# Writing the product of gate and up into up's PSUM bank, and rounding both of its halves from there

## What is computed

```python
x = x + attn(layernorm(x), Wq, Wk, Wv)
z = layernorm(x)
shared = (silu(z @ sg.T) * (z @ su.T)) @ sd.T
probs = sigmoid(z @ router_w.T + routing_bias)         # top 2 of 8, scores normalised
g, u = silu(z @ gate_w[e]), z @ up_w[e]                # for each expert e
out = x + shared + sum_e w[:, e] * ((g * u) @ down_w[e])
```

## Time and profile before

| | us |
|---|---|
| median of 3 runs | 566.49 |
| lowest, highest | 561.99, 566.75 |
| span of the profiled execution | 555.3 |
| what lies around the span (median minus span) | 11.2 |
| TensorE matmuls busy | 518.0 (93%) |
| VectorE busy | 369.8 (67%) |
| ScalarE busy | 301.0 (54%) |
| GpSimd busy | 288.9 (52%) |

### The profile page before, as it was taken

The page is one execution under the profiler, slowest core; times in us unless marked ns, Lnnn a source line. Parts: engine busy times, 40 slices in busy tenths (PEclk is TensorE's granted clock), DMA queues, the critical chain, the costliest instruction groups (busy, mean ns, idle before and its releaser), DMA issues.

```text
span 555.3 us, 14903 instructions
## 1 busy us (share of the span) xinstructions
PE 518.0 (93%) x4757; PEld 425.5 (77%) x4757; DVE 369.8 (67%) x980; ACT 301.0 (54%) x580; POOL 288.9 (52%) x242
## 2 busy tenths in 40 slices
PE   4889988999999999997999999999999999999992
PEld 3557766788878888886767788888787888888881
DVE  5788998689887878899747555445454454454551
ACT  3989877678777676744233443433343433434341
POOL 4466677668676765857022344452444434434443
PEclk9999999899999999998899999999999999999998
DMA  8799848949694947414465965764846536345443
GB/s 271 201 181 208 178 127 158 217 133 209 161 208 141 194 127 170 155 70 136 131 115 85 98 107 69 103 83 60 108 59 89 73 60 97 55 65 78 62 58 38
DMA packets 139351, 68.55 MB, mean 123 GB/s; under 512 B 114608, under 2 KB 132336, under 8 KB 139280
## 3 DMA queue, kind: packets, MB, share of 16 engines
q1 hardware_dynamic: 126128, 48.84, 43.5%
q0 software_dynamic: 13152, 18.76, 19.4%
HBM read 19.46 MB, written 23.08 MB: 77 GB/s over the span
## 4 chain that ended last, share of the span: by engine, by line
PE 65%; DVE 12%; DMA 8%; SPq 5%; ACT 5%; issue 3%; POOL 1%; POOLq 0%; ACTq 0%; DVEq 0%
PE bank L2216 29%; PE bank L2240 15%; PE bank L2547 4%; PE bank L2322 3%; PE bank L2564 3%; DMA v<-xnrow 2%; PE bank L2625 2%; PE bank L2347 2%; PE bank L2392 2%; DMA xn2t<-xrow 2%; PE bank L2369 2%; PE bank L2640 2%; SPq L405 2%; DMA x<-x 1%; DVE h L1470 1%
## 5 line engine op out<-in xcount | busy, mean ns | idle before, releaser
L2216 PE MATMUL bank<-xn2t,w 128*128 128x256 f16 x1608 | 184.9, 273 | 1.3 <-DVE th L1653 1.1
L2216 PEld LDWEIGHTS bank<-xn2t,w 128*128 (+1 forms) x1608 | 155.2, 98 | 24.3 <-DVE th L1653 2.2
L1644 DVE SCALAR_TENSOR_TENSOR th<-th,bank 128x512 f32<-128x512 f32 x83 | 56.6, 682 | 55.2 <-ACT th L989 54.1
L2240 PE MATMUL bank<-w,h 128*128 (+1 forms) x768 | 91.5, 273 | 0.0
L943 ACT ACTIVATE h<-th 128x512 f16<-128x512 f32 (+1 forms) x69 | 42.9, 622 | 84.6 <-DVE th L1653 78.3
L989 ACT ACTIVATE th<-bank 128x512 f32<-128x512 f32 x83 | 49.2, 593 | 62.1 <-PE bank L2216 47.6
L2240 PEld LDWEIGHTS bank<-w,h 128*128 128x128 f16 x768 | 74.0, 98 | 10.4 <-DVE x L1676 0.3
L866 POOL DMA_INDIRECT out<-p,wm x28 | 43.9, 1569 | 67.2 <-ACT p L1323 27.3
L1470 DVE TENSOR_TENSOR h<-th,h 128x512 f16<-128x512 f32 (+1 forms) x69 | 50.6, 733 | 38.3 <-ACT h L943 38.1
L734 POOL TENSOR_TENSOR w<-wst,w 128x768 f16<-128x768 f32 x36 | 59.1, 1645 | 18.9 <-ACT w L943 18.7
L758 POOL DMA_INDIRECT rows<-xrow,sidx x56 | 56.5, 1009 | 17.0 <-issue 13.3
(11 more groups left out here) (188 smaller groups left out, 808.4 us busy)
## 6 DMA issues: line engine op xcount, KB each, us to landing
wst<-w_all SPq DMA_DIRECT2D x36, 384.0 KB
x<-x SPq DMA_DIRECT2D x8, 512.0 KB, 5.6
out<-x SPq DMA_DIRECT2D x8, 512.0 KB, 4.0
rows<-xrow POOLq DMA_DIRECT2D x1, 1192.5 KB, 6.6
rows<-xrow,sidx POOLq DMA_INDIRECT x56
out<-p,wm POOLq DMA_INDIRECT x28
xn2t<-rows SPq DMA_TRANSPOSE x26
wm<-rows SPq DMA_DIRECT2D x26, 9.0 KB, 2.4
```

The source lines that it names most:

```text
L1644: d.scalar_tensor_tensor(out=tb, in0=tb, scalar=1.0, in1=G[half][:, :], op0=ALU.add, op1=ALU.mult).then_inc(f_sg, 1)
L2216: ins = mm(dst, w_ap(j, ws, m * MAT + k * I + (2 * half + i) * P, P), moving(ms * KD + k), start=(cnt == 0), stop=(cnt == 3 * KD - 1))
L2240: ins = mm(o[:, a * D:(a + 1) * D], hb[:, (hs * KI + i) * TT + a * P:(hs * KI + i) * TT + (a + 1) * P], w_ap(j, ws, 2 * MAT + i * D, D), s ...
```

## The change

`ffn_up` writes the product to `U[half]`, in place, and `split_h` and `ffn_low` read it there. So `th[half]` is free after `f_h`, and `tanh` waits for `f_h` of half n - 2. `U[half]` is free only after `f_lo`: TensorE waits for it before the first matmul into `U` (the wait for `f_h` before `G` stays where it was), and before the value projection. The second half of the last pair waits for `f_lo` too, and keeps its product in `th`; singles and halves are as before.

```diff
@@ -985,7 +985,7 @@
                 if isinstance(t, int) and t < 0:
                     return
                 act.wait_ge(gu_mm, t * 2 + half + 1)
-                wait(act, f_lo, t * 2 - 2 + half + 1)
+                wait(act, f_h, t * 2 - 2 + half + 1)
                 a.activation(th[:, half * 512:(half + 1) * 512], G[half][:, :], ACT.Tanh,
                              scale=0.5 / WS).then_inc(f_tanh, 1)
 
@@ -999,7 +999,7 @@
                     act.wait_ge(dump_in, 16)
                 wait(act, dn_mm, t * 2 - (4 if shared else 2) + half + 1)
                 copy((h_of_tile(t) if shared else h)[:, half * 512:(half + 1) * 512],
-                     th[:, half * 512:(half + 1) * 512]).then_inc(f_hi, 1)
+                     U[half][:, :]).then_inc(f_hi, 1)
 
             def ffn_half(t, half):
 
@@ -1650,8 +1650,8 @@
                     return
                 tb = th[:, half * 512:(half + 1) * 512]
                 dve.wait_ge(f_sg, t * 2 + half + 1)
-                d.scalar_tensor_tensor(out=tb, in0=tb, scalar=0.5 / (WS * WS), in1=U[half][:, :], op0=ALU.mult,
-                                       op1=ALU.mult).then_inc(f_h, 1)
+                d.scalar_tensor_tensor(out=U[half][:, :], in0=tb, scalar=0.5 / (WS * WS), in1=U[half][:, :],
+                                       op0=ALU.mult, op1=ALU.mult).then_inc(f_h, 1)
 
             def ffn_half(t, half):
 
@@ -1664,7 +1664,7 @@
                     return
                 ht_ = h_of_tile(t) if isinstance(t, int) else h
                 dve.wait_ge(f_hi, t * 2 + half + 1)
-                low(ht_[:, (2 + half) * 512:(3 + half) * 512], th[:, half * 512:(half + 1) * 512],
+                low(ht_[:, (2 + half) * 512:(3 + half) * 512], U[half][:, :],
                     ht_[:, half * 512:(half + 1) * 512]).then_inc(f_lo, 1)
 
             def add_shared(t):
@@ -2206,6 +2206,8 @@
                     pe.wait_ge(f_h, t * 2 - 2 + half + 1)
                 for m in mats:
                     o = (G[half], U[half])[m]
+                    if m == 1:
+                        wait(pe, f_lo, t * 2 - 2 + half + 1)
                     for i in range(2):
                         dst = o[:, i * TT:(i + 1) * TT]
                         if shape3:
@@ -2359,7 +2361,7 @@
                     pe.wait_ge(xn0_lo, KD)
                     pe.wait_ge(wv_lo, 1)
                 for m in range(first, last):
-                    wait(pe, f_h, 4 * (b - 3) + 3 + m)
+                    wait(pe, f_lo, 4 * (b - 3) + 3 + m)
                     if b:
                         pe.wait_ge(v_lo, 2 * b - 1 + m)
                     for i in range(2):
@@ -2695,7 +2697,7 @@
 
             def last_gate_up(t, j, moving):
 
-                pe.wait_ge(f_h, t * 2)
+                pe.wait_ge(f_lo, t * 2)
                 pe.wait_ge(ys_read, SINGLES)
                 pe.wait_ge(yh_read, HALVES)
                 for i, banks in enumerate(LAST_CHUNKS):
```

## The result

The changed kernel takes 579.33 us (median of 4 runs, 577.61 to 583.10), the kernel before 564.24 us beside it (4 runs, 560.76 to 566.75): ratio **1.0297, interval 1.0242 to 1.0351**. The forecast was 578.0 us, slower.

The account below looks back on a forecast made before the run. TensorE was taken to bound the routed stage, VectorE the end of the shared stage. Opening 0 + middle 1.0 + end 8.8 + clock 1.7 = 11.5 us, on a 555.3 span with 11.2 around it: 578.0 us, range 569.5 to 584.

Parts of the forecast that it names:

- absorbed: Rival: at the end of the shared stage VectorE hides most of TensorE's lateness; +4.1 us, 570.6 us, chance 0.16.
- faster: Rival: low parts no longer collide with GpSimd operations, giving back 5.5 us; 561.0 us, chance 0.06.
- the clock falls at each new wait: Rival: three drops of TensorE's clock at 2.5 us each on the chain; 583.8 us, chance 0.08.
- The end of the shared stage, step by step: Six steps following how U's waits for low parts delay TensorE and VectorE from half 22 on; +8.8 us.
- step 5: Low part of half 28 takes 0.69 us, ending +4.3; VectorE's addition after tile 13's down product starts +8.6.
- Steps 1 to 4: End of shared stage: U of halves 22, 24, 26, 29 late by 0.86, 3.8, 6.1, 8.65 us; table of quads +7.7.
- the sum's +1.7: TensorE's clock: +1.7 us taken between one drop less (-2.5) and three more (+7.5).
- The opening: U of half 2 comes 3.2 us later, half 3's low part gives back 2.06; 0 taken, bounds -0.7 to +1.6.
- The middle of the stage: Middle of the shared stage: U waits in three batches, losing 0.31, 0.37 and 0.32 us; together +1.0 us.
- The routed stage: TensorE bounds it; at least 2.81 us of room per half hides the price; over 1 us longer would be wrong.
- The median of the runs leaves 11.2 us around it, which stay: Base of the forecast: profiled span 555.3 us, median 566.49; the 11.2 us outside the span remain unchanged.
- The signs it named: New profile: U of half 24 4.8 us later, TensorE idle some 10 us, singles table near 270, low parts under 0.8 us.

Follow-up runs that it names:

- e2: Kernel before with the product kept in SBUF, but TensorE waiting for the low part before U and the value projection: 582.70 us, ratio 1.0419.
- e6: The change for halves 20 to 31 alone, the other halves as in the kernel before: ratio 1.0340.
- e7: Changed kernel with five low parts earlier in VectorE's list and one high part earlier in ScalarE's: ratio 1.0037 to the kernel before.
- e9: Changed kernel with TensorE repeating G's matmuls ahead of the waits at halves 24, 26, 29 and 30: 575.57 us, ratio 1.0205 to before.
- e4: The change for the shared expert's 32 halves alone, routed ones as in the kernel before: 580.25 us, ratio 1.0381.
- e11: Changed kernel with low parts of halves 22, 23 and 24 earlier on VectorE and one high part earlier on ScalarE: ratio 1.0181 to before.
- e10: Changed kernel with GpSimd making the low parts of weight chunks 32 and 33 after batch 7's last four scatters: ratio 1.0220 to before.
- e12: Changed kernel with only the low parts of halves 27 and 28 earlier in VectorE's list: ratio 1.0181 to the kernel before.
- e1: The kernel before, unchanged, run for a second profile: 563.5 us, ratio 0.9961.
- e3: The change for the routed experts' 51 halves alone, shared ones as in the kernel before: ratio 0.9964.
- e8: Kernel before, product in SBUF, with five low parts earlier in VectorE's list and one high part earlier in ScalarE's: ratio 1.0000.

## Why the prediction was right

It forecast a loss by the later release of U, at the end of the shared stage, and the runs show that: e2 has the cost with the waits alone, e6 has it with the last twelve halves alone, and e7 loses it again by moving low parts. The rivals "absorbed" (570.6) and "faster", where low parts no longer collide (561.0), are out. Of the rival "the clock falls at each new wait" (583.8) half is true: three drops came in this stage, but they cost 4.8 us and not 7.5. The time came within 1.3 us, but that close by luck, as the paragraph "Around the span" shows.

**The end of the shared stage, step by step.** e9 is the changed kernel without clock drops there, so it shows the steps by themselves. Shifts are against the kernel before, less the shift of U(20) (5.4 us after, 4.4 in e9):

| point | predicted | e9 | after |
|---|---|---|---|
| U(22) | 0.9 | 0.9 | 1.3 |
| U(24) | 3.8 | 3.8 | 4.3 |
| U(26) | 6.1 | 6.0 | 6.5 |
| U(29) | 8.65 | 8.6 | 10.6 |
| table of quads starts | 7.7 | 8.1 | 11.0 |
| U(30) | 10.5 | 14.4 | 17.3 |
| add_shared(14) | 8.8 | 12.8 | 18.0 |
| U(32) | 10.5 | 12.0 | 17.2 |

(U(30) by step 5: 258.8 + 0.06 - 248.38 = 10.5. U(32) is 8.8 + 1.7 for the clock.) Steps 1 to 4 hold within 0.4 us. **Step 5 failed**: "at 0.69 it ends at 250.37 + 7.7 + 0.69 = 258.8" took the collision for a property of the low part. It belongs to GpSimd's two operations, whose place comes from GpSimd's own list. In all six kernels that are late there (after, e2, e4, e6, e9, e11) they met an operation of the table; in e7, e10 and e12, where the table was done before they began, no operation of VectorE was held up. In e9 it was:

```profile
260.63 3.86 DVE L1773 SCALAR_TENSOR_TENSOR phl<-phl,tneg 1x18 f32<-1x18 f32 x1
```

3.86 - 0.23, its time without a collision (e10), is 3.6 of the 3.9 us by which U(30) is later than forecast. This is a sum; the experiment on it, e10, was spoilt.

**The clock.** The drops behind the new waits came, and cost more than forecast. No run shows the sum's +1.7: it was the author's estimate, between no other figures than multiples of 2.5 us, by which 24 matmuls at a granted clock of 0.50 (5.30 us) last longer than 24 at 1.00 (2.79 us at 284.54 after). Between e9 and after lie 5.2 us (18.0 - 12.8 at add_shared(14)). Of these, 0.5 stand at U(22) already, before the first drop; the other 4.8 are what the drops cost. The prediction also counted on 2.5 us for a drop of the kernel before that would go. It went (granted clock 1.00 from 284.54 to 287.33), but gave back only 0.8, from 18.0 to 17.2 in after and from 12.8 to 12.0 in e9. The first routed gate-up tells why. Before:

```profile
266.20 5.70 PE L2216 MATMUL bank<-xn2t,w 128*128 128x256 f16 x48
```

and after:

```profile
289.17 5.41 PE L2218 MATMUL bank<-xn2t,w 128*128 128x256 f16 x48 [1.84 <-issue]
```

At a granted clock of 1.00 the down product is over sooner (2.79 us against 5.30), but TensorE then waits 1.84 us: the gate-up starts 4.69 us after VectorE's addition ends, against 5.16 with the product at 0.50, and is itself 0.3 us shorter. So the clock's net term is 4.8 - 0.8 = 4.0 us where the sum had 1.7. The step that failed is "nearer to where the new idle times fall short of the 3.14 that the row shows": idle times of 2.25 and 2.29 us were followed by a drop here.

**The opening** was put at 0; it costs 2.7 us (35.5 or 35.6 in the eight profiles with the whole change there, 32.7 to 33.1 in the five without), over its bound of 1.6. U(2) is 3.2 us late as forecast, after an idle time of 3.01 us, and then runs at a granted clock of 0.50 (67.80 to 71.10):

```profile
67.80 5.74 PE L2218 MATMUL bank<-xn2t,w 128*128 128x256 f16 x36 [3.01 <-DVE h L1470]
```

36 matmuls in 5.74 us instead of the 4.10 that such a row takes at 1.00 (233.01 to 237.11): 1.6 us. "Some 1.6 us for what follows it" had no clock in it. 3.2 + 1.6 - 2.05 for the collision is the 2.7 us. "With its full operand in PSUM it should not" is what the traces show: in the kernel before, two low parts whose full operand is a bank took 0.69 us each within a GpSimd operation (the one at 20.55 in 20.25 to 21.90, that at 28.19 in 27.75 to 29.88). Of the two collisions there, that of the low part is won (2.05 us by e2), and the one of `one_hot` stays (2.42 us in both kernels).

**The middle of the stage**: 1.0 forecast. U(4) to U(20) averages 115.3 in the five profiles without the change there (before, e1, e3, e6, e8) and 116.7 in the nine with the new waits, +1.3 (+0.9 without e1), with single ones from 113.8 to 118.0: in agreement, but no closer than that.

**The routed stage** took nothing, as forecast: 0.8 us more from U(32) to the end than in the kernel before, e3 level with e1, 693 ns for the up product.

**Around the span.** "The median of the runs leaves 11.2 us around it, which stay": only 1.8 us lie around it. On the profiled execution as its base the sum would have been 555.3 + 1.8 + 11.5 = 568.6, on a typical one of before (564.24) 575.7. The measured loss is 15.1 us where the steps gave 11.5; of the 3.6 us too few, 2.2 were made up by a first median (566.49) that lay above the later one. That is why the time came out so close. And 15.1 is itself on the small side, for the kernel before was slower beside the changed one (564.24 us) than in the later sets (559.93 to 563.43). e4, whose profile is that of the changed kernel, lost 580.25 - 561.21 = 19.0 us, and from U(0) to U(32) the profiles of after and e4 take 233.0 and 234.2 us against 211.1 to 213.0 in before, e1, e3 and e8, some 21 us. The steps gave little more than half of that: step 5, the clock and the opening are what they lack.

**The signs it named.** No low part takes over 0.8 us (the longest 0.69), the routed stage and the up product stay within their limits. TensorE's idle time ended by low parts came to more than the "some 10 us", 13.8 on the matmul queue alone, and 17.5 with the two called "issue" ahead of halves 22 and 24; the table of singles starts at 284.4 and not near 270.

## What to carry to other kernels

Freeing one buffer early by holding another longer is a trade in release times: compare, for both buffers, when the next user arrives and when the last reader is done. Where a wait is added, first look at the list of the engine that ends it: here the same change cost 3.0% with the low parts where they were and 0.4% with five of them (and one high part) moved ahead of work that could wait, as the kernel before with the same order shows (1.0000). Price a collision by the engine that causes it, not by the operation on which it shows: GpSimd's two operations here last 3.24 us, and held up the low part in the kernel before (4.12 us) and a table operation after (3.62 us). And price a loss of clock by what waits behind it: 2.5 us lost in a product were worth 0.8 where another wait stood next.

## What the runs showed of the hardware

- TensorE's granted clock fell to 0.50 after idle times of 2.25 to 3.01 us and not only after 3.14; also after 2.11 (e12, before 263.10), 2.08 (e8, before 314.14) and 1.84 (e1, before 216.32), where the 0.50 set in up to 0.9 us after TensorE's start (windows of e12 from 264.00, of e8 from 315.00, of e1 from 216.50: 0.50). It didn't always: half 24 came out of 2.52 us at full clock after the change, in e2 and in e6, and at half clock in e4, e10 and e12 (36 matmuls in 4.10 us after the change, and in 5.77, 5.77 and 5.76 in e4, e10 and e12); and half 26 came out of 2.26 us at full clock in e2 and e12 (12 matmuls in 1.48 us at 1.00). With idle times of 1.21 us and less (e9) or 0.67 and less (e7) ahead of these halves it stayed at 1.00.
- A VectorE operation on one partition and 7 elements took 3.62 us, and one on 18 elements with a single SBUF input (L1774 in e11) 3.87, beside two GpSimd operations of 1.6 us each, with which both ended.
- VectorE's write of 128x512 float32 to PSUM instead of SBUF cost 9 ns; ScalarE's read from PSUM instead of SBUF saved 32.
- The waits marked "remote" of 1.95 to 4.58 us ahead of the addition of tile 12 remain unexplained.
